# Where the second pair's projections and the led-in units stand in PSUM: one bank pair and one bank moved in a fused FFN, attention and FFN kernel

## The reference

```python
x = x + 0.5 * ffn(layernorm(x))      # first phase
x = x + attn(layernorm(x))           # q, k, v of the first phase; the loop; Wo in the third phase
x = x + 0.5 * ffn(layernorm(x))      # third phase
# ffn:  h = relu(x @ W_fc.T)**2;  y = h @ W_proj.T;  a 5-step spiking count of y, divided by 5
# attn: 16 heads of width 16, rotary turn of q and k, causal softmax, probs @ v, @ Wo.T + bo
```

## Time and profile before

| | us |
|---|---|
| median of 3 runs (lowest to highest) | 1331.09 (1330.83 to 1335.95) |
| the profiled execution's own time | 1329.68 |
| its span in the trace | 1328.0 |
| PE busy | 1250.2 (94%) |
| DVE busy | 1098.4 (83%) |
| ACT busy | 886.5 (67%) |
| POOL busy | 256.0 (19%) |

### The profile page before, as it was taken

How to read it: one execution, slowest core, us unless ns; L and a number is a source line. 1 busy time by engine, 2 the same in 40 slices (tenths; PEclk the granted TensorE clock), 3 DMA queues, 4 the chain that set the end, 5 groups by cost and what they waited for, 6 DMA issues and landing times.

```text
span 1328.0 us, 22227 instructions
## 1 busy us (share of the span) xinstructions
PE 1250.2 (94%) x8224; PEld 761.0 (57%) x8224; DVE 1098.4 (83%) x2592; ACT 886.5 (67%) x1229; POOL 256.0 (19%) x205
## 2 busy tenths in 40 slices
PE   5999999967899999999999999999999989999996
PEld 5888888944444444434444444444344336988996
DVE  4567777787699999999999999999999844777876
ACT  6766666521277777777777777777777777566654
POOL 5003333442210210120210201101101122222300
PEclk9999999978799999999999999999999989999998
DMA  3124444973481350530710901703501140344311
GB/s 134 41 72 151 151 152 135 176 224 103 100 117 32 53 87 11 84 55 11 117 23 10 138 10 27 113 10 49 90 11 48 44 119 27 106 133 134 97 33 64
DMA packets 87701, 109.26 MB, mean 82 GB/s; under 512 B 25292, under 2 KB 59852, under 8 KB 85964
## 3 DMA queue, kind: packets, MB, share of 16 engines
q1 hardware_dynamic: 87592, 107.83, 34.9%
HBM read 64.09 MB, written 41.68 MB: 80 GB/s over the span
## 4 chain that ended last, share of the span: by engine, by line
PE 73%; DVE 16%; ACT 5%; issue 3%; SPq 2%; DMA 1%; DVEq 0%; POOL 0%; ACTq 0%
PE m_ps L1196 21%; PE o_ps L1234 19%; PE s_ps L1218 7%; DVE maxes L1131 6%; PE yps_c L697 5%; PE ups_a L678 5%; PE ups_c L678 5%; PE yps_a L697 4%; DVE masked L1134 4%; PE gps_a L744 3%; PE gps_c L729 2%; PE gps_a L729 2%; ACT probs L1109 1%; DMA kT<-qkT_parts 1%; PE tps_a L722 1%
## 5 line engine op out<-in xcount | busy, mean ns | idle before, releaser
L1109 ACT ACTIVATE probs<-s_ps 128x1024 f32<-128x1024 f32 (+3 forms) x640 | 538.7, 896 | 191.6 <-PE s_ps L1218 190.6
L1131 DVE TENSOR_REDUCE maxes<-m_ps 128x1 f32<-128x512 f32 x768 | 495.1, 684 | 45.3 <-PE m_ps L1196 33.8
L1196 PE MATMUL m_ps<-kT,qT 64*128 64x512 f32 (+3 forms) x1280 | 415.0, 431 | 28.3 <-DVE maxes L1134 10.1
L1196 PEld LDWEIGHTS m_ps<-kT,qT 64*128 64x128 f32 x1280 | 194.1, 186 | 351.0 <-DVE maxes L1131 194.3
L1218 PE MATMUL s_ps<-qT,kT 64*128 64x512 f32 (+3 forms) x1280 | 307.3, 395 | 7.1 <-ACT probs L1109 6.9
L1234 PE MATMUL o_ps<-probs,v_w 128*32 128x512 f32 (+3 forms) x2560 | 302.4, 545 | 0.2 <-POOL probs L1078 0.2
L1134 DVE CUSTOM_DVE_ANT_0 masked<-m_ps,mask 128x128 f32<-128x128 f32 (+3 forms) x512 | 227.8, 482 | 10.2 <-PE m_ps L1196 8.6
L1078 POOL TENSOR_SCALAR_AFFINE_SELECT probs<-probs 128x512 f32<-128x512 f32 x128 | 82.4, 644 | 640.1 <-ACT probs L1109 640.1
L1218 PEld LDWEIGHTS s_ps<-qT,kT 64*128 64x128 f32 x1280 | 163.5, 187 | 36.9 <-ACT probs L1109 32.9
L572 DVE TENSOR_TENSOR h_lo_a<-hsq_a,h_hi_a 128x512 fp32r<-128x512 f32 x64 | 52.0, 812 | 61.5 <-ACT hsq_a L375 40.0
L1234 PEld LDWEIGHTS o_ps<-probs,v_w 128*32 128x32 f32 x2560 | 50.6, 108 | 72.6 <-issue 59.8
(11 more groups left out here) (136 smaller groups left out, 1899.1 us busy)
## 6 DMA issues: line engine op xcount, KB each, us to landing
qT<-qkT_parts SPq DMA_DIRECT2D x96, 128.0 KB
kT<-qkT_parts SPq DMA_DIRECT2D x48, 256.0 KB
qkT_parts<-qk_hi_a SPq DMA_DIRECT2D x32, 256.0 KB, 4.5
qkT_parts<-qk_lo_a SPq DMA_DIRECT2D x32, 256.0 KB, 4.7
sumsT<-osum SPq DMA_DIRECT2D x32, 256.0 KB, 2.6
table_a<-in_rot SPq DMA_DIRECT2D x8, 768.0 KB, 7.0
xin_a<-in_x SPq DMA_DIRECT2D x8, 512.0 KB, 3.6
xres_a<-in_x SPq DMA_DIRECT2D x8, 512.0 KB, 4.7
```

The source lines that it names most:

```text
L1109: act.activation(probs[:, b % PBUF, 2 * hp:2 * hp + 2, off:CH], s_ps[hp][:, :, off:CH], ACT.Exp, scale=D ** -0.5).then_inc(exp_done, 1)
L1131: last = dve.tensor_reduce(out, m_ps[:, i % MB, 0:width], AX.X, ALU.max)
L1196: last = pe.matmul(m_ps[:, i % MB, at:at + width], qT[n % 2][r0:r0 + HR, j, hp, t * P:(t + 1) * P], kT[n % 2][r0:r0 + HR, hp, k * CH:k * C ...
```

## The change

In words. For chunks 5, 6 and 7 (`c >= NC - 3`) the k products go to `tps` in place of `gps`; PE no longer waits for q's `turn_done` before them, and the v products wait for q's `turn_done` in place of k's. As `tps` is then read by DVE's k turn, PE's next transpose into `tps` (slot 5) waits for that. From it = 8 on PE issues k at slot 1 and v at slot 3, one slot earlier each; DVE reads q at slot 1 in place of 0 for it = 9 and 10, and k at slot 3 as before. The units that are led in go round four banks in place of three: the fourth is `o_ps`, which is idle until the first products with v. From g = 0 on it is three banks again, beginning with bank 0, and unit i waits for the last unit before it in its bank. PE's first product with v waits until the last led-in unit in the fourth bank is read. `masked`, where DVE writes the masked tile, gets a fourth buffer.

```diff
+    def pair_bank(c, x):
+        return tps if x == 1 and c >= NC - 3 else gps
...
         def turn_pair(c, x):
+            bank = pair_bank(c, x)
...
-                dve.tensor_tensor(turned[:, m], gps[:, :, :], table[:, c % 2, m:m + 2, :], ALU.mult)\
+                dve.tensor_tensor(turned[:, m], bank[:, :, :], table[:, c % 2, m:m + 2, :], ALU.mult)\
                    .then_inc(s["turn_done"], 1)
...
-            if first and f in (0, 3) and has(it, 3):
-                turn_pair(it - 3, f // 3)
+            if first and f == (1 if it > NC else 0) and has(it, 3):
+                turn_pair(it - 3, 0)
+            if first and f == 3 and has(it, 3):
+                turn_pair(it - 3, 1)
...
         def project_pair(c, x):
+            bank = pair_bank(c, x)
             if x == 0:
                 wait(pe, "mid_evac", c + 1)
                 wait(pe, "v_evac", c)
-            else:
+            elif bank is gps:
                 wait(pe, "turn_done", 4 * c + 2)
...
         def project_v(c):
-            wait(pe, "turn_done", 4 * c + 4)
+            wait(pe, "turn_done", 4 * c + (4 if pair_bank(c, 1) is gps else 2))
...
             if first and f == 5 and has(it, 2):
                 wait(pe, "mid_norm", it - 1)
+                if has(it, 3) and pair_bank(it - 3, 1) is tps:
+                    wait(pe, "turn_done", 4 * (it - 3) + 4)
                 turn(xm, "mid_T")
...
-            if first and f == 2 and has(it, 3):
+            if first and f == (2 if it < NC else 1) and has(it, 3):
                 project_pair(it - 3, 1)
-            if first and f == 4 and has(it, 3):
+            if first and f == (4 if it < NC else 3) and has(it, 3):
                 project_v(it - 3)
...
+LED = sum(g < 0 for g, _ in ORDER)
+BANK = [i % (MB + 1) if i < LED else (i - LED) % MB for i in range(len(ORDER))]
+BANK_AHEAD = [max([k for k in range(max(0, i - 2 * MB), i) if BANK[k] == BANK[i]], default=-1) for i in range(len(ORDER))]
+LAST_LED = max(i for i in range(LED) if BANK[i] == MB)
...
+    def bank(i):
+        return o_ps if BANK[i] == MB else m_ps[:, BANK[i], :]
...
         def free_bank(e):
-            wait(pe, max_read, ITEM[e] - MB + 1)
+            wait(pe, max_read, BANK_AHEAD[ITEM[e]] + 1)
...
+                if n == j == 0:
+                    pe.wait_ge(max_read, LAST_LED + 1)
```

More of the change, by code:

```diff
@@ L743, in project_pair @@
                                                  ((proj_hi, mT_hi), (proj_hi, mT_lo), (proj_lo, mT_hi))]):
-                    last = pe.matmul(gps[:, ab, :], wt[:, k, n0:n0 + P], x_[:, k, :],
+                    last = pe.matmul(bank[:, ab, :], wt[:, k, n0:n0 + P], x_[:, k, :],
                                      start=(i == 0), stop=(i == 3 * EC - 1))
@@ L1130, in unit @@
                 if k < j:
-                    last = dve.tensor_reduce(out, m_ps[:, i % MB, 0:width], AX.X, ALU.max)
+                    last = dve.tensor_reduce(out, bank(i)[:, 0:width], AX.X, ALU.max)
                 else:
-                    last = dve.tensor_tensor_reduce(masked[:, i % MB, at:at + width], m_ps[:, i % MB, at:at + width],
+                    last = dve.tensor_tensor_reduce(masked[:, BANK[i], at:at + width], bank(i)[:, at:at + width],
                                                     mask[:, CH - width:CH], 1.0, NEG, ALU.add, ALU.max, out)
@@ L1157, in shift_out @@
             wait(dve, shift_in, SHIFTS * step_no(e[1], e[2]))
-            dve.tensor_copy(shiftT[:, :], m_ps[0:2 * G * T, i % MB, 0:P]).then_inc(max_read, 1)
+            dve.tensor_copy(shiftT[:, :], bank(i)[0:2 * G * T, 0:P]).then_inc(max_read, 1)
         pending = []
@@ L1195, in unit @@
             for t, hp, k, width, at in parts:
-                last = pe.matmul(m_ps[:, i % MB, at:at + width], qT[n % 2][r0:r0 + HR, j, hp, t * P:(t + 1) * P],
+                last = pe.matmul(bank(i)[:, at:at + width], qT[n % 2][r0:r0 + HR, j, hp, t * P:(t + 1) * P],
                                  kT[n % 2][r0:r0 + HR, hp, k * CH:k * CH + width], start=True, stop=True)
@@ L1203, in turn_shift @@
             pe.wait_ge(neg_step, 3 * step_no(e[1], e[2]) + 3)
-            pe.transpose(m_ps[0:2 * G * T, i % MB, 0:P], negparts[:, :, :].rearrange("p a c -> p (a c)"), ident[:, :])\
+            pe.transpose(bank(i)[0:2 * G * T, 0:P], negparts[:, :, :].rearrange("p a c -> p (a c)"), ident[:, :])\
               .then_inc(max_done, 1)
@@ L1313, in build @@
     memory = Memory(nc, feed)
-    for n, shape in (("masked", [P, MB, CH]), ("maxes", [P, 2, 2, G // 2, T, NJ]), ("negmax", [P, G * T]), ("negparts", [P, 2, G * T]),
+    for n, shape in (("masked", [P, MB + 1, CH]), ("maxes", [P, 2, 2, G // 2, T, NJ]), ("negmax", [P, G * T]), ("negparts", [P, 2, G * T]),
                      ("shiftT", [2 * G * T, P])):
```

## The result

| | before | after |
|---|---|---|
| median of 7 runs (lowest to highest), us | 1333.93 (1330.83 to 1337.3) | 1319.46 (1318.76 to 1326.72) |
| ratio of the runs, 95% interval | | 0.9903 [0.9882, 0.9923] |
| profiled execution's own time, us | 1329.68 | 1320.66 |
| span, us | 1328.0 | 1318.9 |
| first led-in unit on PE, us | 274.25 | 275.62 |

Faster, by 0.97% [0.77, 1.18]. The forecast was 1320.5 us, with a range from 1314.5 to 1326. The last three rows divide the 9.1 us between the two spans: the tail is 11.45 us shorter, the first unit came 1.37 us later, and the rest took 1.0 us more. The late first unit is not of the change: PE's last up product of chunk 7, ahead of every instruction that was edited, starts at 257.14 us where it started at 255.55.

What follows compares the result with a forecast made beforehand. Before the first scores DVE and PE take turns, then PE bounds. 11.15 us of DVE waits less 1.2 at the hand-over gives 10.0 off 1329.68, so 1319.7; taken as 1320.5 for the median, range 1314.5 to 1326.

Steps and rivals of the forecast that it cites:

- Where the time is: From first unit to first scores, DVE and PE take turns; from 288.4 us DVE waits 16.7 us for units.
- Chunk 5: worth 0: At it = 8, v starts some 3 us earlier but the DMA behind it is untouched: worth 0.
- What each block leaves: DVE's waits behind projection blocks of chunks 6 and 7: 5.55 us left of 16.7, so 11.15 come off.
- left 7.5: Upper bound of DVE's remaining waits in us, with all projection blocks of chunks 6 and 7 slow.
- The q turn at slot 1: DVE's q turn for chunks 6 and 7, one slot later: worth 0 in itself, lies beside k's products.
- The new wait before chunk 7's transposes: PE's wait at slot 5 before transposing chunk 7 is met when PE comes to it: costs nothing.
- The hand-over: At item 69, return to three banks delays the scores by two units: minus 1.2 us, bounds 0.6 and 1.4.
- Behind the scores all moves along: From the first scores PE is the bound; time to the end stays within 2 us of 972.8.
- The clock of the tail: Rival: before the first scores, fewer gaps let PE keep 2.4 GHz; gain 14.4 us, 1315.3 to 1316.7; chance 0.17.
- rival 2: At chunk 7, POOL and ACT become the wait, with slow blocks: about 1325 to 1326 us; chance 0.20.
- rival 3: From the first scores the loop starts at the lower clock, ending slower, about 1338 us at 0.79; chance 0.06.
- The signs that were named: On DVE, largest wait behind q of 7 near 2.7 us, total below 7; no PE stop over 2 during turns.

Runs made afterwards that it cites:

- e8: The kernel after with chunk 5 as before the change (k in gps at slot 2, v at slot 4): 1319.56 us, ratio 0.9884.
- e3: The kernel after with DVE's q turn back at slot 0 for chunks 6 and 7: 1322.84 us, ratio 0.992.
- e1: The kernel after with three banks for the led-in units, keeping k in tps and the new slots: 1328.0 us, ratio 0.9953.
- e4: The kernel after with the three banks beginning at bank 1, so item 69 waits for item 65: 1318.99 us, ratio 0.9893.
- e10: The kernel after with chunk 7's q and v blocks in halves and the three banks beginning at bank 1: 1316.44 us, ratio 0.9869.
- e7: The kernel after with chunk 7's q and v and chunk 6's q halved, earlier transposes and spike steps, hand-over at bank 1: 1314.85 us, ratio 0.9845.
- e2: The kernel after with k back in gps and all slots as before, keeping four banks for led-in units: 1329.05 us, ratio 0.9963.
- e6: The kernel after with two spike steps of chunk 7 moved earlier, into DVE's wait for the first units' DMA: 1322.21 us, ratio 0.9895.

## Why the prediction was right

By its own steps:

- **Where the time is.** Right. DVE is at the same place 14.2 us behind the first unit before and 14.1 after, and the gain is DVE's waits: they are 12.25 us less, and 0.7 us more of its own work lies ahead of the scores, which makes the 11.45 to a tenth. The columns of the experiments show that this adds up with other waits left in it.
- **Chunk 5: worth 0.** Right for the tail (e8); for the time of the first unit the runs leave it open.
- **What each block leaves.** Forecast and measured: k of 6 0 and 0, v of 6 0.35 and 0, q of 7 2.7 and 2.34, k of 7 1.0 and 0, v of 7 1.5 and 2.11. The sum 5.55 was 4.45. k of 7 missed by the clock: its block ran at the upper level and took 3.06 us (322.13 to 325.19), as the clock had risen during q of 7 and not fallen since. v of 7 erred the other way, all 24 matmuls at the lower level (5.42 us). I took 4.4 and 4.9 for all. The errors are -0.35, -0.36, -1.0 and +0.6, so they cancel only in part, and a mean was a fair price for the sum and a poor one for each term. The upper bound of the sum, "left 7.5", is 8.0 by the prediction's own terms (0.85, 3.4, 1.7 and 2.0); the range does not hang on it.
- **The q turn at slot 1: "worth 0 in itself".** Wrong as a step, though not in the sum. e3 shows that undoing it costs about 2.5 us of waits (its tail is 3.2 us longer). I had worked out k of 6 with the turn already moved, and so booked at zero what it was that moved k of 6: PE's wait for `negparts` is 2.30 us after, 4.21 before and 5.03 in e3.
- **The new wait before chunk 7's transposes: nothing.** Right: no wait of DVE's follows them. In e1, with three banks and the transposes at the lower clock, they themselves leave 1.62 us.
- **The hand-over: minus 1.2.** Right in kind, and in size within what the runs give. Undone, it moves 1.1 us of DVE's work behind the scores in e4 and 1.9 in e10; before to after it is 0.7.
- **Behind the scores all moves along.** Right: 973.8 against 972.8. It had an end that I did not see: e7 shows that some 9 us further the next load is in the way.
- **The rivals.** The clock of the tail did not come back (0.73). ACT's copy of `mT_hi` of 7 ended at 311.57, 1.5 us before DVE asked for it, so rival 2's margin was right. The loop began at 0.94, so rival 3 did not occur. The signs that were named came out: the largest wait is the one behind q of 7, the total is below 7 us, and PE's longest stop before a unit beside a turn is 1.15 us, at 327.05.

The tail's sum was 10.0 and is 11.45, 1.1 us of waits less than forecast and half a microsecond less for the hand-over; 1.37 us later at the first unit and 1.0 at the end bring the two profiled executions to 9.0. The medians of seven lie 14.5 us apart, the ratio says 12.9 [10.3, 15.7]: before's runs scatter over 6 us, and its profiled execution was one of the fastest. From one execution of each side alone the gain would have been read 4 us too small. That the forecast of 1320.5 us lies only 1 us from the median is luck in part: it took 10.6 us off a median of three of 1331.09 us, where the median of seven is 1333.93 and the ratio gives 12.9.

## What to carry to other kernels

Where two engines hand tiles to each other in order, count for each long block on the producer what the consumer has in hand when it begins: buffers ahead times the consumer's time for one, plus its other work that lies there. What is left over is the wait, and it can be worked out for each remedy and each set of remedies (a buffer more, a block moved beside other work, a block cut in halves) before any is built. The gains of single remedies are not to be added: here 5.0 and 3.0 us alone made 11.45 together. Then ask of every transfer behind the stretch how much sooner it will be wanted.

## What the runs showed of the hardware

The same 12 matmuls of 512 columns took from 2.75 us in the middle of the first phase through 3.06 (k of 7 in after) to 5.42 (k of 7 in e1), and the same 24 of 256 columns from 2.88 to 5.42, by which of the two clock levels PE had at that moment, 2.4 or 1.2 GHz. The clock of the tail did not follow the longest stop of PE in it: behind the first unit that is 2.30 us in after, at a clock of 0.73, 4.21 us in before, at 0.76, and 5.03 us in e2, at 0.73. Two kernels that differ only in where item 69 stands got other levels for the same block: q of 7 took 4.56 us in after and 5.24 in e4, while v of 7 left a wait of 2.11 us in after and none in e4.

DVE's 1.14 us step with two SBUF operands took 2.2 us on average beside POOL's subtraction and adds (6.72 for three, e6) and POOL's pair of adds 4.46 in place of 2.50, where instructions of DVE that read PSUM kept their time beside POOL: in after the units at 307.53 us their 0.61 beside its adds, and the turn at 330.69 us its 2.33 beside its subtraction (330.13 to 332.51).
